# Two attention rounds to a cycle: all units behind the second round, its maximum and exponential issued early

## What is computed

```
xn = layernorm(x)
u  = conv4(xn @ W_in + b_in); y = recurrence(u, tanh(A), Bp, Cp, Dp)
a  = silu(y) @ W_out + b_out
q, k, v = split(xn @ W_qkv + b_qkv)                      # 16 heads of 16
attn = softmax(q k^T / 4) v
gate = softmax(xn @ W_gate + b_gate); top 2 of 8
moe  = sum_e gate_e * (xn @ W_experts[e] + b_experts[e])
out  = x + a + attn + moe
```

## Time and profile before

| | before |
|---|---|
| median of 3 runs | 829.98 us (825.52 to 832.55) |
| the profiled execution's own time | 831.9 us, span 830.1 us |
| mean granted TensorE clock | 0.967 |
| PE busy | 783.4 us, 94% |
| DVE busy | 583.2 us, 70% |
| ACT busy | 530.0 us, 64% |
| POOL busy | 391.2 us, 47% |

### The profile page before, as it was taken

How to read it: one execution, slowest core, us unless ns; L and a number is a source line. 1 busy time by engine, 2 the same in 40 slices (tenths; PEclk the granted TensorE clock), 3 DMA queues, 4 the chain that set the end, 5 groups by cost and what they waited for, 6 DMA issues and landing times.

```text
span 830.1 us, 13136 instructions
## 1 busy us (share of the span) xinstructions
PE 783.4 (94%) x4368; PEld 450.1 (54%) x4368; DVE 583.2 (70%) x834; ACT 530.0 (64%) x916; POOL 391.2 (47%) x531
## 2 busy tenths in 40 slices
PE   8799989998999999999999999999999999999995
PEld 6356555555555655555555655565555554554542
DVE  4567866976679756886568866797668967578720
ACT  3436756775666756667467756767667765766764
POOL 6534644563345723456235634456235453343542
PEclk9769999999999999999999999999999999999997
DMA  8401101122010311102211031113111111112100
GB/s 273 88 2 41 39 5 37 40 67 63 20 42 18 86 44 40 37 5 74 56 40 41 12 86 34 39 39 90 40 40 40 37 55 26 44 31 64 34 2 26
DMA packets 32497, 39.30 MB, mean 47 GB/s; under 512 B 8639, under 2 KB 18661, under 8 KB 32430
## 3 DMA queue, kind: packets, MB, share of 16 engines
q1 hardware_dynamic: 31102, 36.71, 16.9%
q0 software_dynamic: 512, 0.95, 0.7%
q10 hardware_dynamic: 816, 0.80, 0.4%
HBM read 8.18 MB, written 4.19 MB: 15 GB/s over the span
## 4 chain that ended last, share of the span: by engine, by line
PE 78%; DVE 14%; issue 3%; DMA 2%; ACT 1%; SPq 1%; POOL 0%; ACTq 0%; POOLq 0%; DVEq 0%
PE PS L421 41%; PE SB L547 13%; PE PS L577 10%; DVE mx L974 10%; PE TB L561 6%; PE PS L471 4%; PE PS L437 2%; DVE ys L830 1%; DVE xl L862 1%; DMA Pt<-in_wvg 1%; DMA kst<-qkl 1%; PE PS L519 1%; PE PS L505 1%; DVE qkl L856 1%; PE PS L433 1%
## 5 line engine op out<-in xcount | busy, mean ns | idle before, releaser
L974 DVE TENSOR_REDUCE mx<-SB 128x2 f32<-128x1024 f32 x256 | 313.0, 1223 | 186.2 <-PE SB L547 185.7
L1028 POOL TENSOR_TENSOR acc<-acc,mt 128x256 f32<-128x256 f32 x320 | 249.0, 784 | 240.7 <-ACT mt L625 155.2
L764 ACT ACTIVATE Pt<-TB 128x1024 f32<-128x1024 f32 x256 | 262.5, 1025 | 40.6 <-PE TB L561 37.5
L625 ACT ACTIVATE mt<-PS,cpad 128x256 f32<-128x256 f32 x256 | 107.5, 470 | 92.7 <-PE PS L421 90.8
L547 PE MATMUL SB<-kst,qst 48*128 48x512 f32 x512 | 130.5, 506 | 22.2 <-DVE mx L974 16.5
L577 PE MATMUL PS<-Pt,V 128*17 128x512 f32 x1024 | 138.7, 614 | 1.1 <-ACT Pt L764 1.1
L547 PEld LDWEIGHTS SB<-kst,qst 48*128 48x128 f32 x512 | 48.4, 186 | 128.5 <-DVE mx L974 64.3
L421 PE MATMUL PS<-weh,xTh 128*128 128x512 f32 x256 | 110.9, 433 | 4.8 <-DVE qkl L856 1.7
L561 PE MATMUL TB<-qst,kst 50*128 50x512 f32 x512 | 105.5, 407 | 3.9 <-ACT Pt L764 3.0
L421 PE MATMUL PS<-wel,xTh 128*128 128x512 f32 x256 | 101.3, 396 | 0.0
L421 PE MATMUL PS<-weh,xTl 128*128 128x512 f32 x256 | 100.8, 394 | 0.0
(11 more groups left out here) (145 smaller groups left out, 1151.7 us busy)
## 6 DMA issues: line engine op xcount, KB each, us to landing
qst<-qkh SPq DMA_DIRECT2D x124, 64.0 KB, 2.2
kst<-qkh SPq DMA_DIRECT2D x124, 64.0 KB, 2.2
out<-acc SPq DMA_DIRECT2D x8, 512.0 KB, 2.9
qst<-qkl SPq DMA_DIRECT2D x62, 64.0 KB, 2.2
kst<-qkl SPq DMA_DIRECT2D x62, 64.0 KB, 2.2
acc<-in_x SPq DMA_DIRECT2D x7, 512.0 KB, 3.8
Bt<-in_wexp SPq DMA_DIRECT2D x2, 512.0 KB, 7.0
raw<-in_wexp SPq DMA_DIRECT2D x2, 512.0 KB, 8.9
```

Source lines behind the costliest of these rows:

```text
L625: return e.activation(mt[:, item % NM, :], P, ACT.Copy, scale=scale)
L764: e.activation(Pt[:, T % NP, :, :], TB[:, :, :], ACT.Exp, scale=0.25).then_inc(s_ex, 1)
L974: e.tensor_reduce(mx[:, g % 2, 0:2, 4 * jj + a], SB[:, :, :], AX.X, ALU.max).then_inc(s_mx, 1)
L1028: e.tensor_tensor(v, v, mt[:, item % NM, :], ALU.add).then_inc(s_mt, 1)
```

## The change

`first(t)` names the steps with `values` (odd t from 13 to 255). The planner still adds their budget but leaves such a step before it places X, P or any unit, and it keeps a positive budget for the following step. So the order on PE is: score, turned scores, values, score, turned scores, units of both steps. PE's own code is unchanged. On DVE the maximum of the second step moves into the first one, behind its convolution tap and ahead of everything else in that step; on ACT the exponential of the second step moves directly behind that of the first. The unit P (turned attention sums) comes two steps later.

```diff
+def first(t):
+    return LAG + 2 <= t < STEPS and (t - LAG) % 2 == 0
+
+def turn_at(g):
+    t = 8 * g + LAG + 9
+    return t + 2 if t < STEPS else t
...
-        spent = min(spent, 0.0) + max(left / max(last - t, 1), vector[t]) - fixed(t)
+        spent = (spent if first(t - 1) else min(spent, 0.0)) + max(left / max(last - t, 1), vector[t]) - fixed(t)
+        if first(t):
+            continue
...
-        g, rest = divmod(t - LAG - 9, 8)
-        if rest == 0 and 0 <= g < NG:
+        for g in [g for g in range(NG) if turn_at(g) == t]:
             row.append(("P", g // 4, g))
...
+            def exponentials(t):
+                T = t - LAG
+                if 0 <= T < STEPS:
+                    e.wait_ge(s_ST, T + 1)
+                    if T >= NP:
+                        e.wait_ge(s_PV, (T - NP) // 2 + 1)
+                    else:
+                        e.wait_ge(s_lo[(W_QK, W_VG, W_IN)[T]], 1)
+                    e.activation(Pt[:, T % NP, :, :], TB[:, :, :], ACT.Exp, scale=0.25).then_inc(s_ex, 1)
...
                 for u in early(t):
                     unit(u)
-                T = t - LAG
-                if 0 <= T < STEPS:
...
+                if not first(t - 1):
+                    exponentials(t)
+                if first(t):
+                    exponentials(t + 1)
...
-                if 0 <= t < STEPS:
+                if 0 <= t < STEPS and not first(t - 1):
                     largest(t)
                 for s in (3, 2, 1, 0):
                     for b, d in y_read(t - s - 1):
                         conv(b, d, s)
+                if first(t) and t + 1 < STEPS:
+                    largest(t + 1)
                 for u in early(t):
                     unit(u)
```

## The result

The changed kernel takes 852.26 us (median of 6 runs, 847.44 to 853.18), the kernel before in the same rounds 829.91 us: a ratio of 1.0265 with a 95% interval of 1.0223 to 1.0307, 22.3 us more. The forecast had the sign and a little under half of the size (840 us).

A forecast was written before the change was run, and what follows sets the result against it. PE's own work was taken to set most of the end, the score-maximum-next score handshake a part; 831.9 - 3 - 16 + 8 + 19 + 2 = 841.9, as a median 840 us, range 816 to 858 (the forecast case's own 832 to 850).

The forecast's parts named there:

- What bounds the kernel, and the first steps: Whole kernel: PE's work sets most of the end, the maximum handshake a part; first steps become 1.82 us, PE alone 1.65.
- Units leaving the first steps: 80 first steps lose their unit to the second step, each saving 0.04 us: -3 us.
- the change of shape: PE going from attention matmuls into a unit and back: 0.2 us; without such a price the sum would be 16 us higher.
- Second steps hardly ever empty: Second steps left without work after a costly Z pair nearly vanish: -16 us, bounds 0 and -18.5.
- No cover for DVE's lateness: First steps without a unit expose DVE's lateness in the crowded stretch of six batches: +8 us, bounds 0 and 28.
- The second maximum passes the rest of its step's DVE work: T's transposes wait about 3 us for normalised rows in six batches, half clock after: +19 us, bounds 0 and +27.
- Exponential moved up: ACT's second exponential: 0.3 us of cover before PE overwrites TB, used up by late unit copies: +2 us (0 to 8).
- `turn_at` at 0: Turn of the attention sums two steps later, only the add and the batch's store waiting behind it: 0 us.
- The sum: All terms added to the profiled 831.9 us: 841.9 us, predicted as 840 us, 1.2% slower.

The follow-up runs named there:

- the run that kept the old place: Kernel before with its plan unchanged, but second maximum and exponential moved up as in the change: 943.99 us, ratio 1.1417.

## Why the prediction was right or wrong

**What bounds the kernel, and the first steps: right.** The 1.82 us of the steps without a unit held as the floor of all 121 (95 lie within 0.03 us of it), and PE's own 1.65 showed as soon as the maximum was short. Units leaving the first steps were to bring -3 us; the table gives -15.5 + 14.4 = -1.1. The prediction also weighed that the change of shape might have no price of its own, and put 16 us on that. For this sum it was too much, since only 3 us of it hung on that price; the rest of the 16 us was to be hidden by the maximum, as it was. They show only where the maximum is short: 5.51 us against 5.32 for a pair.

**Second steps hardly ever empty: right.** -16 us forecast, -8.5 - 7.2 = -15.7 in the table; some 1 us of the 8.5 stood behind a T step and not behind a step without a unit. Two empty second steps remained.

**No cover for DVE's lateness: right where it was forecast, but that was not the whole.** +8 us forecast for the crowded stretch, +13.9 measured in all. The two first steps ahead of each T step, which lie in that stretch, are late by 7.5 us in the changed kernel and by 8.2 with the second maximum back in its step. So this part belongs to the pairing. (Its size, 1.3 us per batch, had been chosen between wide bounds; that it came so near is partly luck.) The rest is lateness in light stretches, 10.1 us against 3.8 before and 3.6 with the maximum put back: the moved maximum's doing, up to 1 us a time behind short second steps. There DVE's remaining work of the pair (gates and the normalised sums) starts only after the second maximum and runs past the next score:

```profile
514.95 0.50 PE L560 MATMUL SB<-kst,qst 48*128 48x512 f32 x2
...
515.81 0.73 DVE L936 TENSOR_TENSOR G<-G,g 128x32 f32<-128x32 f32 x1
...
516.47 1.21 DVE L993 TENSOR_REDUCE mx<-SB 128x2 f32<-128x1024 f32 x1
...
517.74 0.50 PE L560 MATMUL SB<-kst,qst 48*128 48x512 f32 x2 [1.07 <-DVE mx L993]
```

**The second maximum passes the rest of its step's DVE work: the step that failed.** The mechanism was right, its price was not. It was put at one reader, the T unit, +19 us, and at nothing everywhere else. The T steps lose 13.5 us more than before, with waits for the normalised rows of 1.4 us on average (7.0 in 5) in place of 3: in three of the six steps other units stand ahead of the transposes. (The forecast also counted two stretches of half clock in the T steps of the kernel before; its trace has one, from 370 to 373 us, and the clock stays at 1.00 behind the shorter waits there.) The moved maximum costs 23.1 us in all, as the run without it showed: 8.9 at the T steps, 9.8 in other second steps, 5.9 in late first maxima, less 1.5. The rest of the T steps' loss, some 4.6 us, is the pairing's own and stays. What I had left out is that every early unit's read and the whole tail of DVE's first step wait for the second score, so that any unit whose bank or operand hangs on them is a reader: Y behind `xl` is the one shown. The term "other second steps" (+13.0) had no line in the sum except 2 us for the exponential; 3.2 of it stay with the maximum put back, with V's wait for `at` among them, and belong to the new plan.

**Exponential moved up:** +2 forecast. Undone, it made the kernel slower by some 2 us, which can't be told from nothing: a loss doesn't show.

**`turn_at` at 0:** no run shows that it costs nothing, since V's waits for P's bank (`at`, 3.1 us in 3) are new in the changed kernel and stay with the maximum put back. Without it P would wait for the copy of the attention sums, 50.6 us in the run that kept the old place.

**The sum:** -1.1 - 15.7 + 13.9 + 13.5 + 13.0 = +23.6 in steps 13 to 254, against a forecast of -3 - 16 + 8 + 19 + 2 = +10. Of the 13.6 us between them, 13.0 are second steps without T, 5.9 lateness and 1.9 the first steps; 0.3 the empty steps; 5.5 too much at T and 2 for the exponential go off.

The 9.8 us of the other second steps are hardly half clock. The Y step shown above loses 3.1 us, 1.8 of them by its longer wait; it is the only one of these steps with a stretch of half clock. The rest are 0.3 to 0.7 us in some 15 steps at full clock. What each of those waits for is still open.

## What to carry to other kernels

An instruction that waits for another engine should not be moved ahead of work on its queue that is ready, unless someone needs its result early: here the next score was a block of units away, and the moved maximum, by holding back the reads behind it, cost 23 us. When a gain is priced as "so much saved per step", look for a step of the kernel before that already has the new form; it showed 1.82 us, not 1.65, and the handshake that limits it has to be shortened before the new form can pay.

## What the runs showed of the hardware

A row maximum over 2 x 256 columns takes 692 ns and over 2 x 512 columns 1223 ns, so 531 ns for 512 columns more and, by the straight line through these two, 160 ns that don't depend on the columns. At the Y unit behind the first Z pair a wait of 2.28 us on PE was followed by 3 us at a granted clock of 0.50 (1.2 GHz), while a wait of 0.45 us at the same place left it at 1.00 (2.4 GHz).
